# Two graph-attention layers rewritten as functions of their own, each with a written-out order, and one with its logit columns made as rows

## The reference, cut to what matters

```python
def gnn0(h0, adj):                       # H = 4 heads of 64
    h = einsum('bnd,hde->bhne', h0, W)
    e = (h @ a_src[:, 0])[..., :, None] + (h @ a_dst[:, 0])[..., None, :]   # adj 0 or 1
    att = softmax(where(adj == 0, NEG, leaky_relu(e, 0.01)))
    dst = einsum('bhij,bhje->bhie', att, h) + bias
    return layernorm_per_head(relu(dst) + h) * gamma + beta

def gnn1(h, adj):                        # one head of 256
    Wh = h @ W
    e = leaky_relu((Wh @ a1)[:, :, None] + (Wh @ a2)[:, None, :], 0.2)
    return elu(softmax(where(adj > 0, e, NEG)) @ Wh)

x = x + gnn0(layernorm(x), adj)
x = x + mamba2_block(layernorm(x))
x = x + gnn1(layernorm(x), adj)
x = x + bidirectional_lstm(layernorm(x))
```

## Time and profile before

| | us |
|---|---|
| median of 3 executions (4829.57 to 4834.06) | 4832.03 |
| the profiled execution | 4839.06 |
| its span | 4837.3 |

### The profile page before, as it was taken

The page is one execution under the profiler, slowest core; times in us unless marked ns, Lnnn a source line. Parts: engine busy times, 40 slices in busy tenths (PEclk is TensorE's granted clock), DMA queues, the critical chain, the costliest instruction groups (busy, mean ns, idle before and its releaser), DMA issues. The chain is left out here.

```text
span 4837.3 us, 142627 instructions
## 1 busy us (share of the span) xinstructions
PE 4119.1 (85%) x55809; PEld 2885.5 (60%) x55809; DVE 3534.2 (73%) x8962; ACT 2911.6 (60%) x7074; POOL 1201.2 (25%) x1028
## 2 busy tenths in 40 slices
PE   7888888888399999999998999975888888888882
PEld 4444444444156666666665788854777777777772
DVE  5888888888388888888887677753666666666666
ACT  5777777777298888888886666641333332333330
POOL 3666666665222222222222000000000000000000
PEclk9999999999699999999999999987999999999996
DMA  2121111111100000000001333331111111111115
GB/s 61 60 63 54 53 62 62 53 53 45 53 23 27 27 27 27 27 23 23 27 27 39 109 119 116 118 108 24 34 40 41 39 37 41 42 34 40 43 30 158
DMA packets 326283, 252.58 MB, mean 52 GB/s; under 512 B 171244, under 2 KB 289772, under 8 KB 323564
## 3 DMA queue, kind: packets, MB, share of 16 engines
q1 hardware_dynamic: 324076, 235.03, 16.8%
q10 hardware_dynamic: 1536, 8.39, 0.6%
HBM read 159.42 MB, written 67.11 MB: 47 GB/s over the span
## 5 line engine op out<-in xcount | busy, mean ns | idle before, releaser
L2309 PE MATMUL lstm_G_psum<-lstm_Whh,lstm_HT 128*32 128x192 f32 x8192 | 440.4, 333 | 268.1 <-DVE lstm_HT L2486 267.8
L847 DVE CUSTOM_DVE_ANT_0 g_S<-g_Z_psum,g_relu 128x512 f32<-128x512 f32 x640 | 438.3, 685 | 301.6 <-ACT g_relu L617 299.7
L617 ACT ACTIVATE g_relu<-g_Z_psum,g_src 128x512 f32<-128x512 f32 x640 | 436.8, 682 | 291.0 <-PE g_Z_psum L463 288.7
L2379 ACT ACTIVATE lstm_TC<-lstm_G_psum 128x192 f32<-128x192 f32 x512 | 170.9, 334 | 708.5 <-PE lstm_G_psum L2309 708.5
L473 PE MATMUL g_PT_psum<-g_ident,g_PR 128*128 128x128 f32 x2560 | 398.9, 279 | 158.3 <-DVE g_PT L855 92.3
L473 PEld LDWEIGHTS g_PT_psum<-g_ident,g_PR 128*128 128x128 f32 x2560 | 301.7, 142 | 354.1 <-ACT g_PR L651 237.2
L1785 ACT ACTIVATE ssm_EX<-ssm_Z_psum,ssm_tok 128x256 f32<-128x256 f32 (+1 forms) x1024 | 372.6, 424 | 155.1 <-PE ssm_Z_psum L1615 85.5
L651 ACT ACTIVATE g_PR<-g_S,g_nmax 128x512 f32<-128x512 f32 x640 | 456.9, 714 | 0.1
L2301 PE MATMUL lstm_G_psum<-lstm_Wih,lstm_XT 128*32 128x192 f32 x8192 | 428.0, 327 | 0.0
L2309 PEld LDWEIGHTS lstm_G_psum<-lstm_Whh,lstm_HT 128*32 128x32 f32 x8192 | 214.2, 109 | 355.2 <-DVE lstm_HT L2486 321.5
L2475 DVE SCALAR_TENSOR_TENSOR lstm_AB<-lstm_TC 128x128 f32<-128x128 f32 x512 | 150.2, 293 | 335.5 <-ACT lstm_TC L2379 331.5
(11 more groups left out here) (266 smaller groups left out, 10614.2 us busy)
## 6 DMA issues: line engine op xcount, KB each, us to landing
g_ADJ<-in_adj SPq DMA_DIRECT2D x64, 1024.0 KB, 5.6
x<-g_XO SPq DMA_DIRECT2D x64, 512.0 KB, 3.4
g_X<-in_x SPq DMA_DIRECT2D x32, 512.0 KB, 4.3
ssm_X<-x SPq DMA_DIRECT2D x32, 512.0 KB, 3.9
x<-ssm_OUT SPq DMA_DIRECT2D x32, 512.0 KB, 2.9
g_X<-x SPq DMA_DIRECT2D x32, 512.0 KB, 3.9
lstm_raw<-x SPq DMA_DIRECT2D x1024, 16.0 KB, 1.8
lstm_U<-x SPq DMA_DIRECT2D x128, 128.0 KB, 3.5
```

The lines of the kernel that those rows point to most:

```text
L617: act.activation(relu[n % 4][:, :], score_bank(b, n)[:, :], ACT.Relu, scale=(1.0 - ALPHA) / ALPHA, bias=src[b.slot][:, t, HH * p + hh:HH * ...
L847: v.tensor_tensor_reduce(S[n % 4][:, :], score_bank(b, n)[:, :], relu[n % 4][:, :], -1.0, 3e38, ALU.add, ALU.min, nmax[:, n % 4:n % 4 + 1] ...
L2309: ins = pe.matmul(bank[32 * j:32 * (j + 1), 0:last - first], HT[t % 2][:, 32 * kc:32 * (kc + 1)], Whh[:, kc, j, first:last], start=False, ...
```

## The change

`attention_phase` is replaced by `first_attention_phase` and `second_attention_phase`. The `pipeline` helper is left to the other phases. In both new functions each engine has a function `period(b)`, a flat list of steps of batches b-2 to b+2 that is repeated, and `at` leaves out the steps of batches that don't exist. The steps themselves are those of before, apart from this:

- First layer: `relu_part(b, 0)` waits for the first part of `split` (`s1`), no longer for the last; the columns lie in bank A1, and `outputs_turned` writes A0 and A1 in turn; `BEFORE` and `DRAIN` say which reader must be done before a bank is written again. `load_x` waits for `xb` and `xn` of the batch whose slot it takes.
- Second layer: `columns` now has `WA` as weights, widened to 32 columns (three copies of the destination vector, then the source vector), and x turned moves. The four node tiles go to four column groups, PSUM partitions 0, 32, 64, 96. `split` then works on 128x128 elements and writes, by four operations on 32 partitions each, the logit rows on the block diagonal of `rows`; `to_tokens` turns the whole once to get the source logits (`sources`). `parts_turned` and `rows_out` are gone. `elu_parts` loses one pass: `high_part` and `elu_sum` take the constants along. `Ob` and `Ab` become four banks Ab. The masks are made per tile.
- Both: the first batch's `norm_stats` comes after the set-up on DVE, not ahead of it.

The steps' instructions and sizes are otherwise the same. The diff, cut:

```diff
-def attention_phase(nc, layer, nb, x_in, adj, weights, consts, x_out, kept=None):
+def first_attention_phase(nc, nb, x_in, adj, weights, consts, x_out, kept):
...
+def second_attention_phase(nc, nb, x_in, adj, weights, consts, x_out):
...
+            def columns(b):
+
+                b.wait(pe, s["xt"], 2, 2)
+                bank_free(b, "co")
+                for kc in range(KC):
+                    for t in range(IT):
+                        ins = pe.matmul(BANK["co"][GROUP * t:GROUP * (t + 1), 0:P], WA[:, kc, :],
+                                        XT[:, kc, t * P:(t + 1) * P], start=(kc == 0), stop=(kc == KC - 1),
+                                        skip_group_check=True)
+                ins.then_inc(s["co_pe"], 1)
+
+            def to_tokens(b):
+                b.wait(pe, s["cols"], 1, 1)
+                bank_free(b, "ct")
+                pe.transpose(BANK["ct"][:, 0:P], cols[:, :], ident[:, :]).then_inc(s["ct"], 1)
...
+            def split(b, stage):
+
+                if stage == 0:
+                    b.wait(v, s["co_pe"], 1, 1)
+                    b.wait(v, s["ct"], 1, 0)
+                    v.tensor_scalar(cols[:, :], BANK["co"][:, 0:P], scales[:, 0:1], None, ALU.mult).then_inc(s["cols"], 1)
+                    v.tensor_scalar(high[:, :], BANK["co"][:, 0:P], scales[:, 0:1], None, ALU.mult).then_inc(s["high"], 1)
+                if stage == 1:
+                    b.wait(v, s["high"], 1, 1)
+                    v.scalar_tensor_tensor(out=rest[:, :], in0=high[:, :], scalar=scales[:, 1:2], in1=cols[:, :],
+                                           op0=ALU.mult, op1=ALU.add).then_inc(s["rest"], 1)
+                    b.wait(v, s["rest"], 1, 1)
+                    v.tensor_copy(mid[:, :], rest[:, :]).then_inc(s["mid"], 1)
+                if stage == 2:
+                    b.wait(v, s["mid"], 1, 1)
+                    b.wait(v, s["z"], IT, (1 - SLOTS) * IT)
+                    for t in range(IT):
+                        g = slice(GROUP * t, GROUP * (t + 1))
+                        ins = v.scalar_tensor_tensor(out=rows[b.slot][g, t * P:(t + 1) * P], in0=mid[g, :],
+                                                     scalar=scales[g, 2:3], in1=rest[g, :], op0=ALU.mult, op1=ALU.add)
+                    ins.then_inc(s["rows"], 1)
...
```

DVE's list in the first layer, which the replay of the prediction walks through:

```diff
+            def period(b):
+                at(b + -1, leaky, 5)
+                at(b + -1, evacuate, 2)
+                at(b + -1, leaky, 6)
+                at(b + -1, evacuate, 3)
+                at(b + -1, leaky, 7)
+                at(b, make_mask, 2)
+                at(b + -2, normalise, 0)
+                at(b + -1, evacuate, 4)
+                at(b + -1, evacuate, 5)
+                at(b + -2, normalise, 1)
+                at(b + -1, leaky, 8)
+                at(b + -2, residual)
+                at(b + -1, leaky, 9)
+                at(b + -2, residual_sum)
+                at(b + -1, evacuate, 6)
+                at(b + -1, leaky, 10)
+                at(b + -1, evacuate, 7)
+                at(b + -1, leaky, 11)
+                at(b + -1, leaky, 12)
+                at(b + -1, evacuate, 8)
+                at(b + -2, squares_sum)
...
+                at(b + -1, leaky, 13)
+                at(b, make_mask, 3)
+                at(b, split, 2)
...
+                at(b + 1, norm_stats)
+                at(b, leaky, 0)
...
+                at(b, leaky, 3)
+                at(b + -1, recip)
+                at(b + 1, make_mask, 0)
+                at(b, evacuate, 0)
+                at(b + 1, make_mask, 1)
+                at(b, leaky, 4)
+                at(b, evacuate, 1)
```

More of the change, by code:

```diff
@@ L417, in _ @@
-            pe.wait_ge(s["setup_v"], 9 if first else 8)
+            pe.wait_ge(s["const"], 48)
+            pe.wait_ge(s["w"], 6 * 16)
+            pe.transpose(Zb[0][0:64, 0:64], arow[:, :], ident[0:64, 0:64])
+            for h in range(H):
+                for kc in range(KC):
+                    into = Zb[1] if h < 2 else PTb[0]
+                    ins = pe.transpose(into[0:E, (h % 2) * D + kc * P:(h % 2) * D + (kc + 1) * P],
+                                       W[:, kc, h * E:(h + 1) * E], ident[:, :])
@@ L611, in relu_part, with rows_out @@
+            def rows_out(b):
+                b.wait(act, s["pt"], 1, 1)
+                b.wait(act, s["z"], ITEMS, (1 - SLOTS) * ITEMS)
+                turned = BANK["pt"][:, :].bitcast(BF16)
+                act.activation(rowsT[b.slot][0:3 * H, :], turned[0:3 * H, 0:N], ACT.Copy).then_inc(s["rows"], 1)
             def relu_part(b, n):
-                p, t, hh = n // (IT * HH), n // HH % IT, n % HH
+                p, t, hh = item(n)
                 b.wait(act, s["z"], ITEMS, n + 1)
@@ L751, in after @@
[L751 to L764 removed]
+                b.wait(act, s["ssq"], 1, 0)
```

1272 lines of the change are left out of this document (693 added, 579 removed).

## The result

| | before | changed |
|---|---|---|
| median of the runs, us | 4830.80 (4827.99 to 4834.06, 4 runs) | 4548.59 (4543.90 to 4549.33, 4 runs) |
| ratio, with its 95% interval | 1 | 0.9414 [0.9397, 0.9430] |
| profiled execution, us | 4839.06 | 4549.33 |

A forecast was written before the change was run, and what follows sets the result against it. No engine was full in the first layer (PE and DVE near 86%); PE bound the second. Gains of 139 us (first layer) and 46 (second) less 2 (ends) made 183, predicting a 4649 us median, range 4610 to 4690.

The forecast's parts named there:

- the ends -2: Start and end of both layers: first statistics behind the set-up, 2 us lost, 8 at most.
- The walk along DVE's list: First layer: DVE's steps laid beside ACT's and PE's at packed cost, all masks slow, giving 32.2 us a batch.
- The low end of the range: First layer at 31.5 us a batch with the second at 15.6, giving 4610 us.
- A perfect order gives about 32: First layer: floor of about 32 us a batch from busy times, a gain of 5 us a batch.
- the stall: First layer: ACT's wait for POOL ahead of the squares, 2.9 us a batch, would fall to about 0.
- columns 0.45: Second layer, PE: 16 column records in four column groups cost 0.45 us, replacing the old columns' 1.70.
- changes of shape 0.18: Second layer, PE: changing the array's shape twice for the new columns costs 0.09 us each, 0.18 together.
- The margin of 2.8 us for DVE against 3.1 for PE: Second layer: DVE empties the bank by its first normalise in 2.8 us; PE needs it after 3.1.
- A: Rival, first layer: new waits replace the old one, 34.7 us a batch, 4719 us; chance 0.13.
- B: Rival, second layer: column groups don't overlap or DVE's longer chain holds PE up, 4695 us; chance 0.07.
- C: Rival, first layer: masks meeting POOL operations' starts take 2.84 us, 39.1 a batch, 4850 us; chance 0.04.
- D: Rival: a wait for the batch before serialises two batches, first layer slower than in C; chance 0.01.

The follow-up runs named there:

- experiment 7: Changed kernel with four more 128x128 transposes a batch on PE in the first layer: 4560.85 us.
- experiment 3: Changed kernel with a phase ahead pairing single POOL and DVE operations; total not meaningful, mask's begin and length beside an addition add up to 2.62 or 2.63 us.
- experiment 8: Changed kernel with item 0 copied out of PSUM twice on DVE in each first-layer batch: 4652.87 us.
- experiment 2: Changed kernel with the first layer's four masks moved on DVE's list beside POOL's two-tensor operations: 4730.36 us.
- experiment 5: Old kernel with the first layer's squares moved on ACT from item 13 to 15, and their sum on DVE later: 4797.29 us, ratio 0.9930.
- experiment 4: Old kernel with the first layer's masks moved from items 4, 5, 6, 8 to 8, 9, 10, 11: 4838.18 us, ratio 1.0014.
- experiment 6: Old kernel with masks at items 8 to 11 and the squares and their sum later: 4802.53 us, ratio 0.9942.
- 10: Changed kernel with the first layer's squares moved on ACT ahead of the exponential of item 9, so ACT waits for POOL: 4604.67 us.
- experiment 13: Changed kernel with normalise(1) ahead of mask 0 in the second layer's list of DVE: 4537.36 us, ratio 0.9388.
- experiment 11: Changed kernel with the second layer's columns made twice over, 32 records instead of 16: 4562.02 us.
- experiment 12: Changed kernel with the second layer's logit columns in the old form, put into the new order: 4582.57 us, ratio 0.9490.

## Why the prediction was wrong, and where it was right

**The sign was right, the size was not.** 282 us against 183, and 4549 lies below the range's 4610. By the forecast's three terms: the first layer 139, measured (37.02 - 29.80) x 30 = 217; the second 46, measured 1.57 x 28 = 44 in full flow; the ends -2, measured about +21, which with the others makes 282.

**First layer, the price of a mask: the step that failed.** The walk along DVE's list took all four masks slow. From start to start a slow one costs 1.3 us (606.69 to 607.99 for that of the earlier trace rows), so they are 5.3 of the 32.2 us; the other steps come to 26.9. The low end of the range, 31.5, took the old mean of 1.16, three slow masks and a fast one. Measured, none is slow: from start to start the four take 0.3 to 0.45 us, 1.5 together. With that the same walk gives 26.9 + 1.5 = 28.4 us, DVE is busy 28.6, and PE's 29.6 become the bound (experiment 7): 29.80 a batch instead of 32.4, which in 30 batches is the 78 us that this term missed. The prediction named a mean near 1.2 as a sign that it is right; it is 0.44. The old mean was an average over two kinds of place, 0.41 in the clear and 1.4 beside an addition, and a new order draws anew from both. The row that shows a slow mask was read rightly as the rest of POOL's operation and 0.3; experiment 3 gives 0.29. Then the walk had to lay POOL's list beside DVE's and ask which kind of operation stands at each mask. The forecast only said that masks meet a busy POOL "at random points". These lists aren't random: in experiment 8 mask 1 meets the same operation batch after batch (over 91 masks the mean is 0.99 us, with one of four at 2.57), and in experiment 2 three masks of four meet one (a mean of 1.92 over 85).

**First layer, the floor.** "A perfect order gives about 32" rested on PE's 32.0 and DVE's 31.8. The text itself called PE's figure an upper bound, and then used it as a floor. DVE's was inflated by the waiting masks and PE's by modelled ends; in the new order, which has few of either, they are 28.6 and 29.6. The forecast's range at its low end, 31.5, kept this false floor, so the measured 29.8 could not lie in it.

**First layer, the stall.** Right that it goes and that 2.9 us of ACT's waiting vanish. It was less of DVE's idle time than the prediction took it for: alone it gave 1.2 us a batch, 34 us in all (experiment 5), and the slow masks gave nothing there (experiment 4). The other 6.2 us a batch came with the new list as a whole; that its mixing of the steps of three batches is what brings them is my reading of the waits in experiment 6. In the new order an added wait costs 0.84 to 1.09 times its length (experiments 2, 8, 10), and in experiments 2 and 8 a slower clock of PE on top.

**Second layer.** Right in most of its terms, and in its sum (16.0 against 16.02) partly by luck: columns 0.45 (0.43), changes of shape 0.18 (0.25), the transpose 0.11 (0.11). The price of the drain that the Trainium skill (TensorEngine Tiling (Array Packing), Key Properties) announces for a change of tiling mode is thus 0.25 us a batch here, far too little to decide. The margin of 2.8 us for DVE against 3.1 for PE was one for the first `normalise`; the second, `normalise(1)`, held PE up by 0.23 us, and moving it gave 0.34. So the steps alone need 15.68 (experiment 13), 0.3 less than the sum, and a stall that the sum didn't have filled the difference.

**Ends.** Forecast as a loss of 2. In the first layer the first reciprocal comes 9.2 us earlier (75.17 against 84.41); what in the fill brings that, no run shows apart. In the second layer the first four batches and the last ones run 12 us shorter than 44 us of steady flow explain: between the first and the fourth columns lie 36.8 us instead of 45.7, and from the last columns to the last output 31.8 instead of 35.0.

**Rivals.** A didn't come: none of the first layer's margins of tenths failed. B fell with experiment 11. C's mechanism is real and its price of 2.84 was right to a quarter of a microsecond (2.61), but it didn't come because the new order keeps every mask clear, by 0.2 us. Experiment 2 is C brought about, with three masks of four: 36.0 us a batch. Its weight of 0.04 stood on a guess about random meeting, not on the two lists. D didn't come.

## What to carry to other kernels

A group's mean hides that an operation has two prices. Before you use it in a new order, split it by what the other engine does at that moment, and lay the other engine's list beside the new one. Take busy time as a floor only after such waits and modelled ends are taken out of it. And a wait or a slow operation has no price of its own: removed from a kernel with idle time on all sides it may give nothing, put into a full one it costs about its whole length, and more where PE's clock falls behind it. A margin of 0.2 us can be worth 100 us.
